# Layer 1 mixing carried tile by tile inside the second edge stage, with quadrant radial products and one PSUM pair for the path weights

## The reference, cut to what matters

```python
xn = layernorm(x)
# edge part: radial net, path weights, messages, sum by destination
r = silu(rbf @ M1); r = silu(r @ M2); r = silu(r @ M3)      # 16 -> 64 -> 64 -> 64
tpw = (r @ M4).reshape(E, 4, 64)                            # "path weights"
m0e = tpw[:,0]*x0*sh0 + tpw[:,3]*einsum(x1, sh1)/sqrt(3)    # x0, x1: rows of up(xn) gathered by src
m1e = tpw[:,1]*x0*sh1 + tpw[:,2]*x1*sh0
msg = segment_sum(m0e, m1e by dst) -> polynomial A -> B -> o, batch norm
# mixing part ("linear attention", 8 heads of 64)
k, v = instance_norm(xn @ Wk), instance_norm(xn @ Wv)       # per node and head
dots = einsum("nd,ne->de", k, v) over all nodes, per head
y = (xn @ Wq) @ dots / n @ Wout + bout
x = x + edge part + y
```

## Time and profile before

| what | us |
|---|---|
| median of 3 runs | 1761.48 |
| lowest, highest | 1757.55, 1762.53 |
| the profiled execution, its own time | 1760.44 |
| its span, first to last instruction | 1758.6 |

### The profile page before, as it was taken

How to read it: one execution, slowest core, us unless ns; L and a number is a source line. 1 busy time by engine, 2 the same in 40 slices (tenths; PEclk the granted TensorE clock), 3 DMA queues, 4 the chain that set the end, 5 groups by cost and what they waited for, 6 DMA issues and landing times.

```text
span 1758.6 us, 31936 instructions
## 1 busy us (share of the span) xinstructions
PE 1411.2 (80%) x9726; PEld 790.2 (45%) x9726; DVE 978.8 (56%) x2349; ACT 563.7 (32%) x1467; POOL 956.9 (54%) x1008
## 2 busy tenths in 40 slices
PE   3578888786787776788879888888888888865999
PEld 1345554454455444453634333333333333453458
DVE  4545555554443333654357666666666666575763
ACT  2233333333333332354123333333333333212420
POOL 0677777777777774000067777777777777300000
PEclk9688888988999887899879999999999999987999
DMA  6433333333333330310033343333333333200001
GB/s 200 103 76 81 81 76 74 87 75 82 76 81 81 76 88 18 121 48 1 0 116 112 110 113 112 111 112 110 112 111 111 113 110 112 73 0 1 1 10 38
DMA packets 77716, 141.26 MB, mean 80 GB/s; under 512 B 24426, under 2 KB 32810, under 8 KB 77096
## 3 DMA queue, kind: packets, MB, share of 16 engines
q0 software_dynamic: 40128, 81.99, 18.4%
q1 hardware_dynamic: 37480, 57.93, 10.9%
HBM read 135.17 MB, written 4.67 MB: 80 GB/s over the span
## 4 chain that ended last, share of the span: by engine, by line
POOL 36%; PE 26%; issue 24%; DVE 6%; DMA 5%; ACT 1%; DVEq 1%; SPq 0%; POOLq 0%; PEldq 0%; ACTq 0%
POOL arena L424 19%; POOL ring L413 17%; DMA ring<-mtab,src 3%; PE ps L1038 3%; PE ps L869 3%; PE ps L1029 3%; PE ps L981 2%; PE ps L727 2%; PE ps L878 1%; PE ps L659 1%; PE ps L740 1%; DMA arena<-utab,src 1%; PE ps L919 1%; DVE arena L1332 1%; DVE small L1056 1%
## 5 line engine op out<-in xcount | busy, mean ns | idle before, releaser
L424 POOL DMA_INDIRECT arena<-utab,src x500 | 473.2, 946 | 354.0 <-DVEq L1292 200.3
L413 POOL DMA_INDIRECT ring<-mtab,src x500 | 481.5, 963 | 203.8 <-issue 196.2
L1168 DVE TENSOR_TENSOR arena<-ps,ring 128x1024 f32<-128x1024 f32 x125 | 153.0, 1224 | 289.9 <-PE ps L727 287.2
L919 PE MATMUL ps<-arena 128*128 128x512 f32 (+1 forms) x386 | 221.4, 655 | 11.8 <-DMA arena<-in_rbf 9.8
L1332 DVE TENSOR_TENSOR arena<-ps,arena 128x768 f32<-128x768 f32 x252 | 228.3, 947 | 0.0
L585 ACT ACTIVATE arena<-ps 128x512 f32<-128x512 f32 x193 | 115.2, 597 | 313.2 <-PE ps L919 310.3
L938 PE MATMUL ps<-arena 128*32 128x512 f32 x1008 | 137.0, 604 | 65.2 <-DVE arena L1332 65.2
L1330 DVE TENSOR_TENSOR arena<-ps,arena 128x512 f32<-128x512 f32 x126 | 87.1, 691 | 140.5 <-DMA arena<-utab,src 117.9
L727 PE MATMUL ps<-arena,ring 128*64 128x128 f32 x2000 | 161.2, 311 | 0.0
L718 PE MATMUL ps<-ring 128*32 128x97 f32 x1000 | 50.0, 274 | 135.0 <-DMA ring<-mtab,src 133.0
L930 PE MATMUL ps<-arena 64*128 64x256 f32 x1016 | 145.6, 406 | 8.9
(11 more groups left out here) (219 smaller groups left out, 1885.2 us busy)
## 6 DMA issues: line engine op xcount, KB each, us to landing
arena<-in_eaT SPq DMA_DIRECT2D x125, 256.0 KB
ring<-mtab,src POOLq DMA_INDIRECT x500
arena<-utab,src POOLq DMA_INDIRECT x500
arena<-in_rbf SPq DMA_DIRECT2D x66, 64.0 KB
ring<-in_fw SPq DMA_DIRECT2D x2, 1024.0 KB, 6.1
utab<-arena SPq DMA_DIRECT2D x1, 2048.0 KB, 7.5
XT<-in_xT SPq DMA_DIRECT2D x2, 1000.0 KB
arena<-in_x SPq DMA_DIRECT2D x1, 1920.0 KB, 9.4
```

The lines of the kernel that those rows point to most:

```text
L413: pool.indirect_dma_start(MR[:, n % 4, k, 0:H], None, mtab, bass.IndirectOffsetOnAxis(ap=src[:, 4 * n + k:4 * n + k + 1], axis=0)).then_in ...
L424: pool.indirect_dma_start(G1[:, n % NSLOT, k, :], None, utab, bass.IndirectOffsetOnAxis(ap=src[:, 4 * n + k:4 * n + k + 1], axis=0)).then_ ...
L919: pe.matmul(ps[:, 0, :], w, x, start=True, stop=True).then_inc(S["s_mlp"], 1)
L1168: dve.tensor_tensor(RM[:, n % 2, :, :, :], ps[:, 1, 0:P].rearrange("p (t q) -> p t q", t=4).unsqueeze(3).broadcast_to([P, 4, KH, WIN]), SW ...
```

## The change

The mixing of layer 1 leaves its place ahead of the edge stage. Its per-tile work becomes `mix1(j, i, q)`, called on PE, ACT and DVE in step q of round i, for the first 16 of the 21 rounds; rounds 17 and 18 carry the masking and the two small weight products; the product with `YT` goes into the layer's tail, between the transposes of the two halves, with an eviction on ACT into `Y1` and two additions into `XT` on DVE. The mixing uses PSUM bank 7. To make room, both path-weight pairs become one (banks 2 and 3), and the segment sums move to bank 4. A radial layer becomes four products of 64x64 weights (16x64 for the first) on the four quadrants of the array with 256 columns each, into two banks; the weights and the input layout follow, and each input block is now loaded by two transfers of 16 rows. k, v and their norms of one tile go through bank 7 one after the other; the sum over tiles moves from PSUM to `KVA` in SBUF. The gathers no longer wait for the mixing. The zeroing of `acc1` now follows the transposes, and the table of spherical harmonics `shv` is loaded ahead of `utab`. PE's rounds are written out; DVE and ACT loop over 15 rounds and write out 6.

```diff
@@ gpsimd
             pool.wait_ge(S["s_utab"], 32)
-            pool.wait_ge(S["s_xt3"], 8)
@@ scalar
+            def mix1(j, i, q):
+                if q == 1:
+                    act.wait_ge(S["s_k1"], j * NT + i + 1)
+                    act.wait_ge(S["s_kvt1"], j * NT + i + 1)
+                    act.activation(K1, ps[:, 7, :], ACT.Copy).then_inc(S["s_k1c"], 1)
+                    act.wait_ge(S["s_v1r"], j * NT + i + 1)
+                    act.activation(SQ1, ps[:, 7, :], ACT.Square).then_inc(S["s_k1q"], 1)
+                if q == 2:
+                    act.wait_ge(S["s_v1"], j * NT + i + 1)
+                    act.wait_ge(S["s_k1r"], j * NT + i + 1)
+                    act.activation(SQ1, ps[:, 7, :], ACT.Square).then_inc(S["s_v1q"], 1)
+                if q == 3:
+                    act.wait_ge(S["s_vnf"], j * NT + i + 1)
+                    act.activation(VS1[:, 0, :], VS1[:, 0, :], ACT.Sqrt).then_inc(S["s_v1std"], 1)
+            def round1(j, i, mixed):
+                for o in range(3):
+                    silu(j, 3 * i + o + 1, 1)
+                    if mixed: mix1(j, i, 2 * o)
+                    collect(j, 6 * i + 2 * o, 0)
+                    silu(j, 3 * i + o + 1, 2)
+                    silu(j, 3 * i + o + 2, 0)
+                    if mixed: mix1(j, i, 2 * o + 1)
+                    collect(j, 6 * i + 2 * o + 1, 1)
@@ tensor, layer
-                pe.matmul(ps[:, 0, :], w, x, start=True, stop=True).then_inc(S["s_mlp"], 1)
+                pe.sem_inc(S["s_step"], 1)
+                for h in range(2):
+                    for g in range(2):
+                        hs = slice(h * H, h * H + k)
+                        mm = pe.matmul(ps[g * H:(g + 1) * H, h, 0:256], w[hs, 0:H], x[hs, g * 256:(g + 1) * 256],
+                                       start=True, stop=True)
+                mm.then_inc(S["s_mlp"], 1)
@@ tensor, weights
-                pe.wait_ge(S["s_prod"], j * NQ + n + 2)
+                pe.wait_ge(S["s_prod"], j * NQ + n + 3)
...
-                        mm = pe.matmul(ps[:, 1 + 2 * quad + h, a * D:(a + 1) * D], R3[hs, c:c + P], m4[hs, :], start=True, stop=True)
+                        mm = pe.matmul(ps[:, 2 + h, a * D:(a + 1) * D], R3[hs, c:c + P], m4[hs, :], start=True, stop=True)
@@ tensor
+            def mix1(j, i, q, r):
+                if r and q < 2:
+                    if q == 0: pe.wait_ge(S["s_kva"], j * (NT + 1) + i + 1)
+                    else: pe.wait_ge(S["s_k1q"], j * NT + i + 1)
+                    for k in range(2):
+                        mm = pe.matmul(ps[:, 7, :], YT[:, k, i * P:(i + 1) * P], wkv1[:, k, 512 * q:512 * q + 512],
+                                       start=(k == 0), stop=(k == 1))
+                    mm.then_inc(S[("s_k1", "s_v1")[q]], 1)
+                if r and q == 4:
+                    pe.wait_ge(S["s_v1n"], j * NT + i + 1)
+                    (four 128x128 products of VN1 and K1 into bank 7) .then_inc(S["s_kvt1"], 1)
+            def round1(j, i, r):
+                for o in range(3):
+                    n = 6 * i + 2 * o
+                    weights(j, n + 1, 1, None)
+                    layer(j, 3 * i + o + 1, 1)
+                    segment(j, n, 0, 2 * o)
+                    mix1(j, i, 2 * o, r)
+                    layer(j, 3 * i + o + 1, 2)
+                    turn(j, n - 1, 1)
+                    weights(j, n + 2, 0, 3 * i + o + 1)
+                    layer(j, 3 * i + o + 2, 0, (o + 2) % 3, i + (o + 2) // 3)
+                    segment(j, n + 1, 1, 2 * o + 1)
+                    mix1(j, i, 2 * o + 1, r)
+                    turn(j, n, 0)
@@ vector, at the end of each step, behind select
+                def mix1(i, q, mixed):
+                    if mixed and q == 1:
+                        dve.wait_ge(S["s_k1q"], j * NT + i + 1)
+                        dve.tensor_reduce(VS1[:, 0, :], SQ1...).then_inc(S["s_k1r"], 1)
+                    if mixed and q == 2:
+                        dve.wait_ge(S["s_v1q"], j * NT + i + 1)
+                        dve.tensor_reduce(VS1[:, 1, :], SQ1...).then_inc(S["s_v1r"], 1)
+                        dve.wait_ge(S["s_v1r"], j * NT + i + 2)
+                        dve.tensor_scalar(vs, vs, 1.0 / 64, EPS, ALU.mult, ALU.add).then_inc(S["s_v1s"], 1)
+                        dve.wait_ge(S["s_v1s"], 2 * (j * NT + i) + 1)
+                        dve.tensor_tensor(VS1[:, 0, :], VS1[:, 0, :], VS1[:, 1, :], ALU.mult).then_inc(S["s_vnf"], 1)
+                    if mixed and q == 3:
+                        dve.wait_ge(S["s_v1std"], j * NT + i + 1)
+                        dve.reciprocal(VS1[:, 0, :], VS1[:, 0, :]).then_inc(S["s_v1s"], 1)
+                        dve.wait_ge(S["s_v1s"], 2 * (j * NT + i) + 2)
+                        dve.wait_ge(S["s_kvt1"], j * NT + i + 1)
+                        dve.tensor_tensor(VN1, ps[:, 7, :], VS1[:, 0, :], ALU.mult).then_inc(S["s_v1n"], 1)
+                    if mixed and q == 5:
+                        dve.wait_ge(S["s_kvt1"], j * NT + i + 2)
+                        dve.tensor_tensor(KVA, ps[:, 7, :], KVA, ALU.add).then_inc(S["s_kva"], 1)
```

More of the change, by code:

```diff
@@ L250, in build @@
         BT = cols(12320)
+        Y1 = cols(8192)
         OT = cols(18432)
@@ L602, in _ @@
                 silu(j, 1, 0)
[L603 to L609 removed]
+                with act.Fori(0, NT - 1) as i:
+                    round1(j, i, True)
+                for i in range(NT - 1, ROUNDS):
+                    round1(j, i, i == NT - 1)
             for i in range(NT // 2):
@@ L613, in _, with back @@
                                ACT.Copy).then_inc(S["s_are"], 1)
-            for i in range(NT // 2):
+            def back(i):
                 c, k = divmod(i, 2)
@@ L617, in _ @@
                 act.activation(BT[:, k, 512 * c:512 * c + 512], ps[:, i % 4, :], ACT.Copy).then_inc(S["s_bte"], 1)
+            for i in range(4):
+                back(i)
+            for i in range(8):
+                c, o = divmod(i, 2)
+                act.wait_ge(S["s_y1"], i + 1)
+                act.activation(Y1[:, o, 512 * c:512 * c + 512], ps[:, 4 + i % 4, :], ACT.Identity,
+                               bias=boc[:, o:o + 1]).then_inc(S["s_y1e"], 1)
+            for i in range(4, 8):
+                back(i)
             for i in range(8):
@@ L956, in _ @@
                 weights(j, 0, 0, 0)
-                with pe.Fori(0, ROUNDS) as i:
-                    for o in range(3):
-                        n = 6 * i + 2 * o
-                        weights(j, n + 1, 1, None)
-                        layer(j, 3 * i + o + 1, 1)
-                        segment(j, n, 0, 2 * o)
-                        layer(j, 3 * i + o + 1, 2)
-                        turn(j, n - 1, 1)
-                        weights(j, n + 2, 0, 3 * i + o + 1)
-                        layer(j, 3 * i + o + 2, 0, (o + 2) % 3, i + (o + 2) // 3)
-                        segment(j, n + 1, 1, 2 * o + 1)
-                        turn(j, n, 0)
+                for i in range(ROUNDS):
+                    round1(j, i, P if i < NT - 1 else LAST if i == NT - 1 else 0)
                 turn(j, NQ - 1, 1)
@@ L992, in _ @@
                 tr.then_inc(S["s_bt"], 1)
-            pe.wait_ge(S["s_are"], 8)
+            for i in range(4):
+                back(i)
+            pe.wait_ge(S["s_Gm1"], npass)
+            for i in range(8):
+                c, o = divmod(i, 2)
+                pe.wait_ge(S["s_are"], i + 5) if i < 4 else pe.wait_ge(S["s_y1e"], i - 3)
+                for k in range(2):
+                    mm = pe.matmul(ps[:, 4 + i % 4, :], GM1[:, k, o * P:(o + 1) * P], YT[:, k, 512 * c:512 * c + 512],
+                                   start=(k == 0), stop=(k == 1))
+                mm.then_inc(S["s_y1"], 1)
+            for i in range(4, 8):
+                back(i)
             for i in range(8):
@@ L1351, in _ @@
                         select(i * ROUND + 8 * o + 8, 3 * i + o + 1, (o + 1) % 3, q % 2)
+                        mix1(i, q, mixed)
+                with dve.Fori(0, NT - 1) as i:
+                    round1(i, True)
+                for i in range(NT - 1, ROUNDS):
+                    round1(i, i == NT - 1)
                 for n in (NQ - 2, NQ - 1):
@@ L1397, in _ @@
                 ins.then_inc(S["s_b"], 1)
+            dve.wait_ge(S["s_y1e"], 8)
+            for k in range(2):
+                link(dve.tensor_tensor(XT[:, k, :], XT[:, k, :], Y1[:, k, :], ALU.add))
             dve.wait_ge(S["s_oe"], 8)
```

219 lines of the change are left out of this document (92 added, 127 removed).

## The result

| kernel | median us | lowest, highest | ratio to the kernel before (95% interval) |
|---|---|---|---|
| before | 1762.01 | 1757.55, 1763.86 | |
| changed | 1842.18 | 1841.41, 1847.5 | 1.0466 [1.0453, 1.0478] |

The change makes the kernel 80 us slower. The direction is the predicted one; the time lies 57 us above the forecast of 1785 and 10 above the range. The profiled execution took 1841.81, its span is 1840.0.

A forecast was written before the change was run, and what follows sets the result against it. Gather issue was taken to bound the second edge stage, 30.0 us a round. From 1760.44, 108.7 gained outside left 1651.7; 16 mixed rounds of 38.7 less 5.5 added 133.7, giving 1785, range 1738 to 1832.

The forecast's parts named there:

- the gain outside: Ahead of the second edge stage and in the tail: 108.7 us saved, 105.3 of it by an earlier first gather.
- hides under the gathers: Rival for the mixed rounds: DVE 29.5 and PE 27.8 stay below 30, giving 1652 us; chance 0.18.
- serial quadrants: Rival for the radial layer: quadrants do not run four at a time, 1827 us, wholly serial about 1900; chance 0.1.
- B: Mixed round, from DVE's products of step 6i+2 to those of 6i+3: 7.30 us, against 5.0 before.
- A: Mixed round, from DVE's products of step 6i to those of 6i+2: 12.97 us, against 10.0 before.
- C: Mixed round, products of step 6i+3 to 6i+4, with table load and root on ACT: 7.52 us.
- D: Mixed round, products of step 6i+4 to 6i+5: DVE's own step, 4.5 us.
- E: Mixed round, products of 6i+5 to 6i+6: adds wait for a turn behind k by v, then PSUM sum: 5.3 us.
- the clock: PE in mixed rounds: some of each may run at 1.2 GHz, taken as 1.1 us a round between 0 and 10.
- the first stop: POOL's one longer stop, at 903.29 near the gathers' start, goes with a shorter radial chain: 1.7 us gained.
- the slack: Three gather slots let DVE be 5.5 us late before POOL stops, taken off the loss.
- 1.2 GHz through the mixed rounds: Rival for PE: half clock throughout the mixed rounds, +10 us a round, about 1945 us; chance 0.04.

The follow-up runs named there:

- the faster kernel: Changed kernel with ACT's mixing pieces ahead of `silu` calls and PE's v and k-by-v products behind the step's own work: 1683.97 us, ratio 0.9561.
- fill experiment: Changed kernel with 288 extra PE products, whose results nothing reads, ahead of `weights` in the mixed rounds: 1785.52 us, ratio 1.0138.

## Why the prediction was right and where it was wrong

**The bound before, and the gain outside.** Right. The first gather is issued at 780.73 (780.8 predicted). That it fits to 0.1 is in part luck: in the traces of the experiments with the same program up to there it comes between 780.7 and 784.7, always 8.4 us behind the issue of `utab`'s store, which itself moves by 4 us. The sum of store and semaphores, 8.4, is what was predicted. The tail's timeline on PE (L1021 is the old L990, L1032 the old L898) has

```profile
1650.07 1.97 PE L1021 MATMUL ps<-small,arena 128*128 128x128 f32 x16 [0.68 <-DVE arena L1456]
...
1651.87 13.90 PE L1032 MATMUL ps<-arena 128*128 128x512 f32 x32
...
1667.27 1.97 PE L1021 MATMUL ps<-small,arena 128*128 128x128 f32 x16 [1.50 <-DVE arena L1456]
```

The product with `YT` fills the idle 15.23 us of the earlier trace rows and the second transposes take 1.97 for 3.67. From the start of the first to the end of the second: 19.17 for 20.86, the 1.7 predicted.

**The mechanism.** Right. The mixing does not hide although the sums of PE and DVE are below 30; order ties the engines into one chain. Without its work the kernel takes 1657, with three calls on ACT moved 1732. The rival "hides under the gathers" left the order out. In the faster kernel it nearly comes true, within 27 us of the kernel without the mixing's work. Its sum for PE (27.8) fits the 343.70 us of 400 that PE is busy there, 27.3 in a round of 31.7; its sum for DVE (29.5) holds queue time that no busy time shows, and stays unchecked.

**The terms of the chain.** The layer was taken at 0.70; it is 0.66 long and 0.60 from start to start at a granted clock of 1.00, so the rival of serial quadrants is out. B was 7.30 and is 7.27. A was 12.97 and is 12.7. C was 7.52 and is 7.55 at full clock. D holds. E was under-sized: 5.3 for 6.39 at full clock. I counted from the turn that stands behind k by v, but had not added up what PE does ahead of it, from `weights(6i+5)` on: weights, layer, segment, k by v, layer, turn, 5.1 us in a row from the end of the products of step 6i+4, and then DVE's adds (1.22), select (0.43) and the sum from PSUM (0.69) ahead of the next products. Moving k by v away brings 5.3. Together the chain is 0.7 longer than summed.

**The step that failed** is the clock: "Between nothing (the 1.00 of the earlier trace rows) and all of it at half speed (+10), I take 1.1, near the low end, because most stretches of the first edge stage are at 1.00." The fill experiment measures 3.8. "Most stretches are at 1.00" was a true reading of the first edge stage and the wrong measure, since it holds for the mixed rounds just as well. Cut into pieces of 4 us, 81 of 123 are at 1.00 in the first edge stage (150 to 642) and 79 of 147 in the mixed rounds (834 to 1422); the means are 0.89 and 0.84. Nor was the first edge stage free of this cost. Its mean is

```profile
150.00:640.00 490.00, 384.51 (x4174) 243.73 (x4175) 226.97 (x605) 172.42 (x557) 371.75 (x389) 0.89 0.33 79
```

and PE has 21 idle pieces of 2.2 to 3.5 us in it, of which the earlier trace rows shows one: a stretch with 1.03 us of PE work in 4, followed by one at 0.50. The mixed rounds have two such pieces each, 3.3 and 2.7, within 10 us. The prediction's own chain had PE idle for about 3 us in each of B and C. The idle piece of B stands ahead of the `weights` of C, that of C ahead of the next one; so B stays at full clock (7.27 in both kernels), and the time lost comes back in C (+1.5) and E (+1.5), and with A in every third round (+1.6).

**Where the 56 us are.** The forecast of 1785.4 was made against a profiled execution, and the changed kernel's took 1841.81, 56.4 more. Up to the first gather nothing of it arises (105.4 gained for 105.3). Behind the last gather 3.7 us are gained where 1.7 were forecast. So from the first gather to the last 58.4 are missing: 190.5 more than before, where 133.7 less the 1.7 of the first stop, 132.0, was forecast. The rounds give 16 x (41.95 less 38.7) = 52.0 of it: about 43 by the clock (3.76 less 1.1 a round) and about 9 by the chain (38.19 less 37.6). The other 6.4 are in the slack and the first stop, for which the forecast took 5.5 and 1.7 off, while of 16 x (41.95 less 30.0) = 191.2 us only 0.8 came off. The trace shows why. The 16 rounds before do not take 30.0 but 29.7 on average, as the first two take only 28.0 and 27.7; the changed ones are therefore 196.1 longer. 2.3 come back ahead of the first products (11.7 us behind the first gather, 14.0 before) and 3.5 in the last five rounds. The single pair has no term of its own here: its cost inside the mixed rounds is part of the chain, and the 4.1 us that it costs the gathers of the kernel before are at most 2.1 in the kernel without the mixing's work.

**What the profile was to show.** Two table loads of 1.28 a round, PE waiting some 3 us for products, and short rounds behind the sixteenth are there. POOL's stops for DVE's products are 209 and not 130; DVE's wait for the root is 3.82 and not 2.2, as `weights` and layer run at half clock ahead of it (2.34 in the fill experiment, where they do not).

**The range** ended at 1832, made with a round of 41.5 and less than half of the clock's upper bound. The clock stood in it as a rival of all or nothing (4% for "1.2 GHz through the mixed rounds", 1945), while the truth lay between the two. That rival's own sum was off as well: it adds the whole 10 to a round of 38.7 that already has 1.1 of them; 47.6 a round gives 1928.

## What to carry to other kernels

Work that fits into every engine's idle time may still not hide. For each piece, write down what stands ahead of it in that engine's program and whom its wait holds up, and put a late piece behind the work the others wait for: three calls moved on ACT and two on PE turned a loss of 80 us into a gain of 78. When a hand-over chain leaves PE idle for about 3 us at a time, price the products behind such a gap at the half clock as well, and take both prices as the bounds. Here that was right behind nearly every gap of 2.7 to 3.3 us in the changed kernel, and too pessimistic with full-width layers, where `weights` still ran at full clock behind 16 of 34 gaps of that kind. The length of the gap alone does not settle it, and a count of stretches at full clock says little.

## What the runs showed of the hardware

- Around idle pieces of 3.34 and 2.69 us the granted clock of PE is 0.50 to 0.60 (1192 to 1204) and `weights` takes 2.08 us for 1.14; at 1208 it is 1.00 again. Products that nothing reads, issued into the idle pieces, hold 1.00 and gave 57 us of 1842.
- A radial layer as four float32 products of 64x64 weights and 256 columns on four quadrants (x8 in the profile) takes 0.66 us, where the full-width product of 512 columns (x2) takes 1.12.
- The quadrants gave 50 us in the changed kernel and 28 in the faster one.
- A table load on ACT takes 1.28 us and starts 0.01 us behind the instruction ahead of it; with a copy in place of the root, and no load, the step is 1.43 shorter.
